# Values of all groups projected once at the beginning and read back from DRAM, with the attention step in another order

## The reference, cut

```python
# B, S, HIDDEN = 4, 256, 512; 32 query heads, 8 key/value heads, HEAD_DIM 128, window 128
xn = layernorm(x)
q, k = rope(xn @ wq), rope(xn @ wk);  v = xn @ wv
scores = q . k * 128 ** -0.5;  allowed = (j <= i) & (j > i - 128)
attn = softmax(where(allowed, scores, min))          # each group: 4 query heads, 1 key/value head
s = (attn @ v) @ wo
W1, W2, W3 = dequant_q40(...)                        # packed 4-bit weights and scales, hidden 1376
g = silu((silu(xn @ W1.T) * (xn @ W3.T)) @ W2.T)
out = x + s * g
```

## Time and profile before

| | us |
|---|---|
| median of 3 timed runs (824.96 to 825.28) | 824.97 |
| the profiled execution, its own time | 827.23 |
| its span, first to last instruction | 824.8 |
| TensorE busy in the span | 813.2 (99%) |
| VectorE / GpSimd / ScalarE busy | 556.8 / 484.5 / 436.3 |

### The profile page before, as it was taken

The page is one execution under the profiler, slowest core; times in us unless marked ns, Lnnn a source line. Parts: engine busy times, 40 slices in busy tenths (PEclk is TensorE's granted clock), DMA queues, the critical chain, the costliest instruction groups (busy, mean ns, idle before and its releaser), DMA issues.

```text
span 824.8 us, 13612 instructions
## 1 busy us (share of the span) xinstructions
PE 813.2 (99%) x4024; PEld 682.1 (83%) x4024; DVE 556.8 (68%) x1640; ACT 436.3 (53%) x1141; POOL 484.5 (59%) x367
## 2 busy tenths in 40 slices
PE   7999999999999999999999999999999999999997
PEld 4888888888878888888888888888888888888886
DVE  5677757653677667584948576766758494858684
ACT  3432312213866738574666666475747465665762
POOL 1232312326666748674675667486748665677997
PEclk9999999999999999999999999999999999999999
DMA  8434322022011101200020102012001201020112
GB/s 243 131 94 149 109 64 84 29 86 77 15 38 37 41 1 52 77 2 25 25 76 0 51 13 64 0 51 67 9 0 51 76 0 51 0 76 0 52 40 102
DMA packets 43594, 44.55 MB, mean 54 GB/s; under 512 B 3492, under 2 KB 28454, under 8 KB 43558
## 3 DMA queue, kind: packets, MB, share of 16 engines
q1 hardware_dynamic: 43264, 44.05, 18.3%
q10 hardware_dynamic: 296, 0.09, 0.1%
HBM read 42.03 MB, written 2.10 MB: 54 GB/s over the span
## 4 chain that ended last, share of the span: by engine, by line
PE 93%; ACT 2%; DVE 2%; issue 1%; POOL 1%; DMA 1%; SPq 0%; DVEq 0%; POOLq 0%; ACTq 0%
PE bank L1198 26%; PE bank L1199 26%; PE bank L1200 26%; PE bank L1312 3%; PE bank L1334 3%; PE bank L1352 2%; PE bank L1353 2%; PE bank L1354 2%; PE bank L1361 1%; PE bank L1359 1%; PE bank L1358 1%; PE bank L1302 1%; PE bank L1208 1%; DVE probs L993 1%; ACT gate L638 1%
## 5 line engine op out<-in xcount | busy, mean ns | idle before, releaser
L1198 PE MATMUL bank<-xh,wih 128*128 128x512 f32 x384 | 155.2, 404 | 0.3 <-DVE k L950 0.3
L1200 PE MATMUL bank<-xh,wil 128*128 128x512 f32 x384 | 150.0, 391 | 0.0
L1199 PE MATMUL bank<-xl,wih 128*128 128x512 f32 x384 | 150.0, 391 | 0.0
L345 POOL TENSOR_TENSOR swap<-swap,cst 128x512 f32<-128x512 f32 x80 | 106.6, 1333 | 67.7 <-ACT swap L575 67.7
L608 ACT ACTIVATE probs<-probs,nmx 128x128 f32<-128x128 f32 x256 | 99.9, 391 | 71.2 <-DVE nmx L975 70.6
L1198 PE MATMUL bank<-woh,oh 128*128 128x512 f32 x256 | 100.3, 392 | 0.1
L1199 PE MATMUL bank<-wol,oh 128*128 128x512 f32 x256 | 100.0, 390 | 0.0
L1200 PE MATMUL bank<-woh,ol 128*128 128x512 f32 x256 | 99.7, 389 | 0.0
L349 POOL TENSOR_TENSOR q<-q,swap 128x512 f32<-128x512 f32 x64 | 91.3, 1427 | 8.9 <-DVE q L950 5.2
L329 POOL TENSOR_TENSOR wil<-raw,wih 128x512 fp32r<-128x512 f32 x48 | 63.5, 1359 | 42.5 <-ACT wih L557 42.5
L369 POOL TENSOR_TENSOR ph<-ph,cst 128x512 fp32r<-128x512 f32 x32 | 42.0, 1312 | 75.3 <-ACT ph L624 75.3
(11 more groups left out here) (119 smaller groups left out, 1922.0 us busy)
## 6 DMA issues: line engine op xcount, KB each, us to landing
raw<-in_wq SPq DMA_DIRECT2D x32, 256.0 KB, 2.8
raw<-in_wo SPq DMA_DIRECT2D x32, 256.0 KB, 2.9
pk<-in_w SPq DMA_DIRECT2D x44, 128.0 KB, 3.5
sc<-in_s SPq DMA_DIRECT2D x36, 128.0 KB, 3.5
pk<-in_w SPq DMA_DIRECT2D x11, 256.0 KB, 2.5
sc<-in_s SPq DMA_DIRECT2D x11, 256.0 KB, 3.2
xn<-in_x SPq DMA_DIRECT2D x8, 256.0 KB, 5.2
raw<-in_wk SPq DMA_DIRECT2D x8, 256.0 KB, 3.1
```

The source lines that it names most:

```text
L345: nc.gpsimd.tensor_tensor(v, v, spread(sin.unsqueeze(1), P, 2, SEQ), ALU.mult).then_inc(sin_done, 1)
L1198: nc.tensor.matmul(out_, sh, mh, start=(i == 0), stop=False)
L1199: nc.tensor.matmul(out_, sh, ml, start=False, stop=False)
L1200: m = nc.tensor.matmul(out_, sl, mh, start=False, stop=(i == n - 1))
```

## The change

The value weights are loaded and split first, and 16 units (8 token tiles by 2 halves of the 1024 value columns) give the values token-major, with no transposes. ScalarE copies the even tiles from PSUM to a staging tile, VectorE subtracts the even from the odd tile, and SP writes both to a DRAM tensor `vals`. In the attention part a half's values of one group are read back into `vraw` and split by one copy and one subtraction. The rows that spread scales go; all weight tiles load their scales. The ring has nine slots, the second feed-forward weights keep six tiles, and the first group's input pieces are split during the feed-forward part. The steps' programs on all engines have another order; out_project 0 now stands ahead of attend 1, and its banks are swapped.

```diff
+        def v_out(pair, half):                                   # ScalarE
+            n = 4 * pair + 2 * half
+            act.wait_ge(vu_ps, n + 1)
+            wait(act, v_odd, n // 2 - 1)
+            wait(act, v_kept[n % 4], 16 * pair)
+            nc.scalar.activation(stage[:, n % 4, :], bank[2 + n % 4][:, :], ACT.Copy).then_inc(v_even, 1)
...
             def v_hi(g, bp):
+                act.wait_ge(v_in[bp], 16 * (g + 1))
                 wait(act, o_ps, cnt(4, g, bp, -4))
+                nc.scalar.activation(vh[:, bp, :, :], vraw[:, bp, :, :], ACT.Copy).then_inc(vh_done, 1)
...
+            def v_step(pair, half):                              # VectorE
+                n = 4 * pair + 2 * half + 1
+                dve.wait_ge(vu_ps, n + 1)
+                dve.wait_ge(v_even, n // 2 + 1)
+                wait(dve, v_kept[n % 4], 16 * pair)
+                nc.vector.tensor_tensor(stage[:, n % 4, :], bank[2 + n % 4][:, :], stage[:, n % 4 - 1, :],
+                                        ALU.subtract).then_inc(v_odd, 1)
...
+            def v_lo(g, bp):
                 dve.wait_ge(vh_done, cnt(1, g, bp, 1))
+                nc.vector.tensor_tensor(vl[:, bp, :, :], vraw[:, bp, :, :], vh[:, bp, :, :].bitcast(f32),
                                         ALU.subtract).then_inc(vl_done, 1)
...
+            def v_unit(n, ahead=None):                           # TensorE
+                i, half = unit(n)
+                pe.wait_ge(xl_done, i + 1)
+                if n >= 4:
+                    pe.wait_ge(v_odd if n % 2 else v_even, 2 * (n // 4) + half - 1)
+                todo = dict(ahead or {})
+                if n in (0, 2):
+                    for d in range(DT):
+                        todo[d] = partial(enough_wv, DT * half + d + 1, todo.get(d))
+                three(bank[2 + n % 4][:, :], [(xh[:, d, cols], xl[:, d, cols], wvh[:, half, d, :], wvl[:, half, d, :])
+                                              for d in range(DT)], todo).then_inc(vu_ps, 1)
...
+            v_unit(0, {2: lambda: x_turn(1)})
+            v_unit(1)
+            v_unit(2)
+            v_unit(3, {1: lambda: x_turn(2), 3: lambda: x_turn(3)})
...
+        def y_bank(g, bp, t):
+            last = isinstance(g, int) and g == NKV - 1
+            return t % 2 if last and (bp == 1 or t == 3) else (t + 1) % 2
...
             def attend(g, bp, b, late=False):
                 for t in range(2):
                     if b == 0:
+                        wait(pe, acc_done, cnt(4, g, bp, t - 1 if late else 0))
                     else:
                         pe.wait_ge(ol_done, cnt(4, g, bp, t + 1))
+                        if late or t:
+                            pe.wait_ge(acc_done, cnt(4, g, bp, t + 1 if late else 1))
...
             def step(g, bp, last):                               # TensorE
+                p_turn(g, bp, 0, 0)
+                p_turn(g, bp, 0, 1)
                 project(ng, nbp, 0)
+                scores(g, bp, 1, 0)
+                scores(g, bp, 1, 1)
                 project(ng, nbp, 1)
                 attend(g, bp, 0)
-                scores(g, bp, 1, 0)
-                scores(g, bp, 1, 1)
                 project(ng, nbp, 2)
                 scores(g, bp, 1, 2)
                 scores(g, bp, 1, 3)
+                project(ng, nbp, 3)
+                project(ng, nbp, 4, {3: lambda: p_turn(g, bp, 1, 0)})
+                p_turn(g, bp, 1, 1)
+                out_project(g, bp, 0)
                 attend(g, bp, 1)
+                scores(ng, nbp, 0, 0)
+                scores(ng, nbp, 0, 1)
                 out_project(g, bp, 1)
                 scores(ng, nbp, 0, 2)
                 scores(ng, nbp, 0, 3)
...
             def step(g, bp, last):                               # ScalarE, from the middle
+                kq_hi(ng, nbp, 0)
+                halves(ng, nbp, 2)
+                kq_hi(ng, nbp, 1)
                 exps(g, bp, 1, 2)
                 exps(g, bp, 1, 3)
+                halves(ng, nbp, 3)
+                kq_hi(ng, nbp, 2)
                 p_hi(g, bp, 1, 0)
                 p_hi(g, bp, 1, 1)
...
             def step(g, bp, last):                               # VectorE, from the middle
+                both(g, bp, 1, 0)
+                kq_lo(ng, nbp, 0)
+                cos_part(ng, nbp, 2)
+                masking(g, bp, 1, 2)
+                kq_lo(ng, nbp, 1)
+                both(g, bp, 1, 2)
                 cos_part(ng, nbp, 3)
                 kq_lo(ng, nbp, 2)
+                p_lo(g, bp, 1, 0)
+                p_lo(g, bp, 1, 1)
                 cos_part(ng, nbp, 4)
+                accumulate(g, bp, 0)                             # finish(0, 0) in the last group
...
             # TensorE, hand-over
+            w2_mult(FT // 2, (0,), (6, 7, 4))
+            pe.wait_ge(ffn_read, place(FT // 2, 7))
             scores(0, 0, 0, 0)
             scores(0, 0, 0, 1)
             project(0, 1, 0)
             scores(0, 0, 0, 2)
             scores(0, 0, 0, 3)
+            w2_mult(FT // 2, (0,), (5,))
...
             # VectorE, hand-over
             cos_part(0, 0, 4)
+            ffn_add(FT // 2, (6, 7, 4))
+            kq_lo(0, 0, 3)
             masking(0, 0, 0, 0)
             kq_lo(0, 0, 4)
             both(0, 0, 0, 0)
             cos_part(0, 1, 0)
+            masking(0, 0, 0, 2)
+            ffn_add(FT // 2, (5,))
```

More of the change, by code:

```diff
@@ L13 @@
 from contextlib import ExitStack
+from functools import partial
 import numpy as np
@@ new lines, in load_wo, with load_v @@
+            def load_wo(slot, g, h):
+                sp.dma_start(raw[:, slot, :], wo[bass.ds(g * (GH * HD) + h * HD, HD), :]).then_inc(raw_in[slot], 16)
+            def load_v(g, bp):
+                wait(sp, vl_done, cnt(1, g, bp, -1))
+                sp.dma_start(vraw[:, bp, :, :], vals_v[:, bp * (IT // P):(bp + 1) * (IT // P), bass.ds(g * HD, HD)]) \
+                    .then_inc(v_in[bp], 16)
+            sp.wait_ge(wvl_done, 2 * DT)
+            for t in range(3, FT):
+                for m in range(2):
+                    load13(t, m)
@@ L252, in _ @@
-            for c in range(6):
-                wait(sp, wl_done, c - RING + 1)
-                load_in(c, 0, c)
+            sp.wait_ge(W2_done, FT)
+            sp.wait_ge(hl_done, 2 * FT)
+            for i in range(4):
+                sp.wait_ge(v_kept[i], 16 * (VU // 4))
+            for bp in range(2):
+                load_v(0, bp)
             def group_loads(g, last):
+                if not last:
+                    load_v(g + 1, 0)
                 for h in range(GH):
                     wait(sp, wl_done, wo_chunk(g, h) - RING + 1)
-                    sp.dma_start(raw[:, (6 + h) % RING, :], wo[bass.ds(g * (GH * HD) + h * HD, HD), :]) \
-                        .then_inc(raw_in[(6 + h) % RING], 16)
+                    load_wo(5 + h, g, h)
@@ L407, in step @@
                 if w:
-                    lo_wo(g, 0)
-                    lo_wo(g, 1)
-                    lo_wo(g, 2)
-                    lo_wo(g, 3)
+                    for h in range(GH):
+                        lo_wo(g, h)
                 if last:
@@ L760, in step @@
                 if nxt:
-                    for c in range(6):
+                    for c in range(5):
                         hi_in(g + 1, c)
@@ L779, in stats, with scales @@
                 nc.vector.bn_stats(stat[:, i, :], xn[:, i, :]).then_inc(stats_done, 1)
-            def scales(part, between):
+            def scales(part, between=None):
                 tiles = PARTS[part]
```

705 lines of the change are left out of this document (317 added, 388 removed).

## The result

The changed kernel takes **843.75 us** (843.01 to 845.13, 4 runs); the kernel before took 824.97 beside it. The ratio is 1.023, with a 95% interval of 1.0212 to 1.0247: 18.8 us slower, where 2.4 us less were forecast. The profiled execution took 845.13, of which 843.3 are its span (before: 827.23 and 824.8).

The account below looks back on a forecast made before the run. TensorE, busy 60.00 of 60 us in the attention loop, was taken to bound the kernel. Terms -6.9 - 7.0 + 5.4 + 4.8 + 1.3 = -2.4 us gave 822.6 us on the 824.97 median; range 814 to 830.

Parts of the forecast that it names:

- start: Kernel's beginning: first tile normalised alone, ninth value unit begins at 38.6 instead of 45.5, 6.9 us gained (5.5 to 9).
- transposes of the values: Attention loop, TensorE: four value transposes per step removed, 0.44 us in each of 16 steps, 7.0 us gained.
- accumulator's bank: Loop: second attention product waits for VectorE's addition of output projection 0's bank, 0.36 us x 15 steps, 5.4 lost.
- late second transposes: Output-weight steps: second probabilities' transposes wait on the GpSimd-ScalarE-VectorE chain, 0.5 x 6 plus 1.8 last group, 4.8 lost.
- hand-over: From feed-forward part to attention: first scores wait for VectorE's reads and masks, 3.0 against 1.7 us, 1.3 lost.
- tail: End of the kernel: TensorE's sequence is as before, 0 (within 0.5 us).
- the 19.0: At the start: time in us taken for the second value unit's end, between 20.4 (all slow clock) and 16.9 (early rise).
- the twin: Last step of the kernel before, which already has the bank wait; its rows gave the price, 0.26 + 0.10 = 0.36 us.
- Hidden transfers: Sixteen stores and reloads of values, 256 KB each, reload issued some 60 us before use: covered, no cost.
- Rival 2: Loop: shared port stretches VectorE operations, transposes late in the other half of steps too; 834, half of that 828; chance 0.13.
- Rival 1: Loop: the late transposes don't occur, 817.8 us; with the bank wait gone too, 812.4; chance 0.25.
- Rival 3: Start gains nothing: late weight pieces or held-back tiles leave the clock slow, 45 instead of 38.6, 829 us; chance 0.13.

Follow-up runs that it names:

- run 7: All reorderings of runs 1, 3, 5 and 6 on the changed kernel, plus last-group residual products and multiplication moved later: 825.30 us.
- run 3: Changed kernel with the copy and subtraction that split a half's values moved to the beginning of the step: 839.97 us.
- run 9: Run 7 with VectorE's masks and multiplications moved earlier, values' split later in first step, GpSimd's four subtractions again ahead of rotation: 826.45 us.
- run 6: Changed kernel with VectorE's order altered only in the hand-over and first step (feed-forward tiles read earlier, masks earlier): 840.08 us.
- run 11: Changed kernel with GpSimd's value-weight subtractions at the start kept apart from the normalising of the first token tiles: 842.23 us.
- run 10: Run 7 with VectorE's masks earlier, key's copy and subtraction in VectorE's idle time (output-weight steps), and first step reordered: 818.82 us.
- run 12: Run 10 with the start edit of run 11: 814.84 us, ratio 0.9884 to the kernel before.
- run 4: Changed kernel with both first scores of the next half put ahead of the second attention product on TensorE: 841.91 us.
- run 1: Changed kernel with the first query's rotation ahead of the last two of GpSimd's four output-weight subtractions: 837.42 us.
- run 2: Changed kernel with last two heads' exponentials ahead of ScalarE's query copy, and their multiplication ahead of VectorE's query subtraction: 838.37 us.
- run 5: Changed kernel with one of the next half's first two scores ahead of the second attention product on TensorE: 837.14 us.

## Why the prediction was wrong

| term | forecast | measured |
|---|---|---|
| start | -6.9 | -5.2 (40.27 against 45.52; this trace) |
| transposes of the values | -7.0 | -6.9 |
| accumulator's bank | +5.4 | +8.5 (12 x 0.63, 3 x 0.31) |
| late second transposes | +4.8 | +19.1 |
| hand-over | +1.3 | +1.8 |
| tail | 0 | +0.9 |
| sum | -2.4 | +18.2 (spans: 843.3 - 824.8 = 18.5) |

The measured column adds what the gaps between TensorE's matmuls have over their usual distance, in each place. Of the 20.6 us between forecast and measurement the late second transposes make 14.3.

*Transposes of the values*: right. In run 7 the step from 298.38 to 333.48 has no wait: 35.10; 38.26 - 12 x 0.2275 - 35.10 = 0.43 each, x 16.

*Late second transposes*: the step that failed, by its size; the chain was the right one. It measured 6 x 1.71, not 6 x 0.5, plus 3.36 in the first group's step and 2.86 in the last, each with 1.6 of fallen clock behind it, less 0.54 that stood there before. Three things were missing. (a) The walk took GpSimd's operations at their length in a trace where little lay beside them; the new value subtraction, which has both inputs in SBUF now, and a multiplication and the key's subtraction stretched them by 1.3 us, more than the slack of the whole chain. Run 3 shows 0.55 of each wait for the values' subtraction, and run 9 gives 0.54, as walked, with the key's subtraction gone too. (The walk's own ends were off as well: 18.6 us, or 19.7 with a multiplication of 1.80, against 18.4 are 0.2 to 1.3 late, not 0.3 to 0.9.) (b) The first group's step was not walked at all; it is an order of its own, and there VectorE's masks were late (run 6). (c) In the last group the residual product was counted, not the fall of the clock. What share the collisions have in (b) and (c) no run separates.

The prediction cites the Trainium skill, page "SBUF — State Buffer", on the port that VectorE and GpSimd share, and let the sum stay. Its section "Who interferes with whom" says that an instruction of VectorE with two tensor inputs in SBUF contends with GpSimd's reads, and that the loser waits for the whole instruction. The trace agrees: 0.69 becomes 1.78, 1.29 becomes 1.75, and 128x1 operations of 0.16 take 1.12 to 1.23. The mistake was to weigh this for one operation and its distance to the next rotation, and not for each such operation beside all of GpSimd's, at the start too.

*Start*: mechanism right, 1.7 us too good in this trace. The second unit ended at 20.64 instead of 19.0, and from there to the ninth it is 19.6, as walked. What the walk lacked is the same collision (three small operations, 3 us together, gone in run 11). Against that, the 19.0 was chosen late: without the collision the second unit ended at 16.96 and 17.72 (the clock rose at 12.4 and 14.7) and the ninth began at 36.59 and 37.35, before the forecast. That 38.6 lies within the 38.37 to 41.79 of the eleven traces is in part luck. *Bank*: right in kind, 0.63 instead of the twin's 0.36: VectorE began the addition 0.12 us after the projection's last row ends and TensorE resumed 0.24 after the addition, against 0.03 and 0.06 in the earlier trace rows. Why these hand-overs are slower stays open. *Hand-over*: right within 0.5. *Tail*: 0.9, where half a microsecond was allowed; TensorE waits there for the split probabilities (0.60) and for the bank (0.17). *Hidden transfers*: right, no wait names a reloaded value.

*Rivals.* Rival 2 named the cause that runs 3 and 9 show for the loop, at 834 and with the wrong place: the half of the steps that was already late became later, while the other half has no wait at the transposes. Rival 1 is what run 10 reaches in the loop, by another order. Rival 3 did not occur.

## What to carry to other kernels

Before work is taken out of a loop, walk every chain that this work covered, and in the walk give each operation the length that it has beside what will lie there, not the length that it has alone: when VectorE reads two tensors from SBUF, a GpSimd operation beside it is one more item in its queue, and the other way round. Moving an input from PSUM to SBUF has a price too: the values' subtraction, placed beside GpSimd's work, cost 3.8 us here (run 3), half of the 7 that the removed transposes gave. Written-out orders have as many places to walk as they have special steps; the first group's step and the last group held 9.4 of the 19.1 us of late transposes here.

## What the hardware showed

- A collision costs much more than its size on short operations: 128x1 operations went from 0.16 to 1.12, 1.17 and 1.23 us. In the thirteen traces of the changed order the first tile's statistics began between 3.45 and 3.63 us, while the first transposes stood at 6.4 to 6.5 (runs 11 and 12), 7.3 to 7.5 or 8.5 to 8.7, by whether none, one or two of the first tile's operations met a GpSimd subtraction (in run 4 the second is the normalising itself, 1.58 instead of 0.54).
- TensorE's granted clock fell to 0.50 for about 3 us behind every wait of 3.1 us in the first group's step (the changed kernel and runs 1 to 5 and 11), which cost 1.6 us on top of the wait. In the last group it fell behind single waits of 2.62 (the changed kernel, runs 4 to 6) and 2.17 (run 3), and in runs 1 and 2 behind two waits in short order, of 1.64 and 0.87 and of 1.81 and 0.88; in run 2 it stayed low for 6.8 us. It did not fall behind the waits of 1.5 in the loop, and in run 11 not behind the same 2.62 either. So the length of a wait alone does not tell here whether the clock falls. Run 11, behind that wait (columns as in the earlier trace rows):

```profile
796.00:800.00 4.00, 4.00 (x22) 3.33 (x22) 3.12 (x5) 2.93 (x6) 3.92 (x4) 1.00 0.00 0
```
